# A third matmul and a ScalarE copy in place of VectorE's add, in the first retention of a two-layer language-model tower

## The reference

```python
h = 0                                   # (128 sequences, 128 tokens, 128)
for k in range(3):                      # taps -1, 0, +1
    src = t + k - 1                     # neighbour's place; zero outside the sequence
    h = h + where(valid(src), conv_w[:, :, k].T[ids[:, src]], 0)
h = h + retention(layernorm(h), Wq, Wk, Wv, ...)   # the phase of this case
h = h + experts(layernorm(h), ...)      # top 2 of 8 experts
h = h + complex_retention(layernorm(h), ...)
h = h + merged_experts(layernorm(h), ...)
```

## Time and profile before

| | |
|---|---|
| median of 3 runs | 2128.21 us (2125.86 to 2129.78) |
| the profiled execution | 2130.03 us, its span 2128.3 us |
| TensorE, matmuls | 1922.6 us busy, 90% |
| VectorE | 1511.5 us, 71% |
| ScalarE | 1330.7 us, 63% |
| GpSimd | 1194.4 us, 56% |
| first retention | from the start to about 690 us |

### The profile page before, as it was taken

One profiled execution on the slowest core, in us unless ns is written; L12 is line 12 of the kernel. 1 busy time (PEld: TensorE's weight loads), 2 busy tenths in 40 slices (PEclk: granted clock), 3 DMA queues, 4 the chain that ended last, 5 costly groups with the idle time before them and its releaser, 6 DMA issues. The chain is left out here.

```text
span 2128.3 us, 59058 instructions
## 1 busy us (share of the span) xinstructions
PE 1922.6 (90%) x19932; PEld 1434.3 (67%) x19932; DVE 1511.5 (71%) x4436; ACT 1330.7 (63%) x2940; POOL 1194.4 (56%) x1544
## 2 busy tenths in 40 slices
PE   5888888888886799999999779999999699999997
PEld 2545544455554577777777657777777599999997
DVE  4978888889886233333333379999998678888877
ACT  3756666666663122222222269999998588899885
POOL 5487887888876677888888711111211033333334
PEclk9999999999996899999999979999999899999999
DMA  3122222122211655555555413111110011111111
GB/s 100 39 63 68 66 65 68 61 68 69 65 50 40 183 163 160 159 160 162 161 163 163 134 65 134 40 39 39 39 39 11 16 36 42 41 41 41 42 41 36
DMA packets 113823, 168.80 MB, mean 79 GB/s; under 512 B 19234, under 2 KB 66747, under 8 KB 113572
## 3 DMA queue, kind: packets, MB, share of 16 engines
q1 hardware_dynamic: 87940, 105.09, 17.6%
q0 software_dynamic: 25760, 62.09, 9.1%
HBM read 121.79 MB, written 45.32 MB: 79 GB/s over the span
## 5 line engine op out<-in xcount | busy, mean ns | idle before, releaser
L1277 ACT ACTIVATE b_hT<-b_hbank,b_w 128x512 f32<-128x512 f32 (+1 forms) x156 | 98.2, 630 | 321.1 <-PE b_hbank L1247 321.1
L1221 POOL DMA_INDIRECT done<-b_y,b_row x270 | 263.5, 976 | 48.8 <-issue 45.0
L353 POOL DMA_INDIRECT sent<-a_xn_mid,a_pos_cur x256 | 258.8, 1011 | 47.1 <-issue 43.6
L1303 DVE TENSOR_SCALAR b_hT<-b_hbank,b_w 128x512 f32<-128x512 f32 (+1 forms) x156 | 105.7, 678 | 223.5 <-PE b_hbank L1247 223.5
L1257 PE MATMUL b_bank<-b_w,b_hT 128*128 128x128 f32 x2160 | 255.9, 277 | 1.0 <-DVE b_hT L1303 1.0
L1257 PEld LDWEIGHTS b_bank<-b_w,b_hT 128*128 128x128 f32 x2160 | 249.1, 193 | 1.2 <-DVE b_hT L1303 1.2
L1247 PE MATMUL b_hbank<-b_xT,b_w 128*128 128x512 f32 (+1 forms) x624 | 246.5, 538 | 0.8 <-ACT b_xT L1284 0.8
L1495 POOL TENSOR_TENSOR c_k_early<-c_xn,const_k_decay 64x512 f32<-64x512 f32 x32 | 40.7, 1272 | 332.1 <-ACT c_xn L1703 332.1
L361 POOL TENSOR_TENSOR tv<-tv 128x64 f32<-128x64 f32 x368 | 136.0, 370 | 67.3 <-DVE a_pos_cur L903 56.3
L1247 PEld LDWEIGHTS b_hbank<-b_xT,b_w 128*128 128x128 f32 x624 | 113.5, 192 | 86.9 <-issue 82.5
L1220 POOL TENSOR_TENSOR b_spacer<-b_fill 128x192 f32<-128x192 f32 x266 | 137.8, 518 | 53.1 <-DVE b_y L1311 42.5
(11 more groups left out here) (249 smaller groups left out, 4487.7 us busy)
## 6 DMA issues: line engine op xcount, KB each, us to landing
b_w<-pack_dram SPq DMA_DIRECT2D x78, 258.0 KB
b_w<-pack_dram SPq DMA_DIRECT2D x78, 256.0 KB, 3.1
c_rows<-done SPq DMA_DIRECT2D x32, 512.0 KB, 3.8
b_x<-sent SPq DMA_DIRECT2D x57, 260.0 KB, 2.7
d_b_all<-b_rows SPq DMA_DIRECT2D x32, 256.0 KB, 3.5
out_dram<-h_all SPq DMA_DIRECT2D x32, 256.0 KB, 2.3
b_b<-pack_dram SPq DMA_DIRECT2D x78, 64.5 KB
tv<-tv_dram SPq DMA_DIRECT2D x1, 4736.0 KB, 16.4
```

What stands on the lines that cost most here:

```text
L353: pool.indirect_dma_start(out=sent_d, out_offset=bass.IndirectOffsetOnAxis(ap=pos_cur[:, g.par, b, k:k + 1], axis=0), in_=xn_mid[:, g.par, ...
L1221: pool.indirect_dma_start(out=done_d, out_offset=bass.IndirectOffsetOnAxis(ap=row[:, s.k, j:j + 1], axis=0), in_=y[:, s.par, j, :], in_off ...
```

## The change

The token's own part is added by a third matmul with the identity matrix, in the same PSUM accumulation, and the sum is only copied to `h_all`. The copy is ScalarE's, in the second place of its step; VectorE's `h_sum` is gone. `h_ready` is now raised by the copy. `normalise` takes the four sequences in reverse order. The gather is untouched: it stays three groups ahead.

```diff
@@ tok (TensorE)
                 nc.tensor.matmul(work[0][:], shift_dn, rows[:, g.par, :, 0:D], start=True, stop=False)
-                nc.tensor.matmul(work[0][:], shift_up, rows[:, g.par, :, 2 * D:3 * D],
+                nc.tensor.matmul(work[0][:], shift_up, rows[:, g.par, :, 2 * D:3 * D], start=False, stop=False)
+                nc.tensor.matmul(work[0][:], ident, rows[:, g.par, :, D:2 * D],
                                  start=False, stop=True).then_inc(tok_made, 1)
@@ ScalarE
+            def h_copy(g):
+                act.wait_ge(tok_made, g.n + 1)
+                nc.scalar.activation(h_all[:, bass.ds(g.n * GB, GB), :], work[0][:].rearrange("p (b d) -> p b d", b=GB),
+                                     ACT.Copy).then_inc(h_ready, 1)
+
@@ normalise
-                for b in range(GB):
+                for b in reversed(range(GB)):
@@ step (ScalarE)
                 if g := s.at(0):
                     k_square(g)
+                if g := s.at(2):
+                    h_copy(g)
                 if g := s.at(0):
                     k_std(g)
@@ VectorE
-            def h_sum(g):
-                dve.wait_ge(tok_made, g.n + 1)
-                v.tensor_tensor(h_all[:, of_group(g), :], work[0][:].rearrange("p (b d) -> p b d", b=GB),
-                                rows[:, g.par, :, D:2 * D], ALU.add).then_inc(h_ready, 1)
-
@@ step (VectorE)
-                if g := s.at(2):
-                    h_sum(g)
```

## The result

| | before | after |
|---|---|---|
| median, same chip | 2127.03 us (2124.74 to 2129.78) | 2149.67 us (2146.85 to 2151.30) |
| the profiled execution, its span | 2130.03, 2128.3 | 2151.07, 2149.4 |
| TensorE, matmuls | 1922.6 busy | 1955.0 busy |
| VectorE | 1511.5 | 1493.2 |
| ScalarE | 1330.7 | 1351.5 |

The changed kernel is slower: ratio 1.0109, 95% interval 1.0093 to 1.0125, 22.6 us by the medians and 21.1 by the spans. In the spans the added time lies here: the first waiting `tok` starts at 113.56 instead of 107.53 (+6.0); the 25 steps from it take 516.7 us instead of 501.9 (+14.8); what follows differs by 0.3 at most.

What follows compares the result with a forecast made beforehand. The prediction took the first retention's loop to be bound by a two-step chain from `tok` through `place_tokens` and the gathers. Start 6.7, loop 5.0 and end 0.9 make 12.6: 2142.6 profiled, 2141 as a median, range 2133 to 2152.

Steps and rivals of the forecast that it cites:

- the forecast's own mechanism: First retention's loop: the third matmul lengthens the gathers' two-step chain by 0.93 a pair; 2137 to 2146, chance 0.46.
- the rival of the clock: Loop: 1.2 GHz stretches behind `tok` stay as frequent or grow; 2147 with six low pairs, 2157 with all; chance 0.24.
- The start, +6.7: Steps before the first bound gather: added matmul and `h_copy`'s table load cost 6.7 us, 3.0 in the first step.
- The third matmul's 0.93 on c: Loop: c, from `tok`'s start (T) to `place_tokens`, grows by 0.93; `q_proj` at T+2.7 to 2.8, `qa` at T+3.8.
- `h_sum`'s removal gains nothing: VectorE's step in the loop: the 0.69 us add sat in a wait for TensorE; gain on the path: nothing.
- `h_copy` is hidden: ScalarE, between `k_square` and `k_std`: the 0.6 us copy ends before `qa` starts, or still ahead of the gate.
- The loop, +5.0: 25 steps: 506.9 instead of 501.9, two pairs of steps at 41.85 and 10.5 at 40.3; waits shrink by about 0.2.
- Low stretches behind `tok` in two pairs: Loop: only the first two gather waits, over 3 us, bring 1.2 GHz behind `tok`; those pairs take 41.85.
- GpSimd gave nothing back: Rival, GpSimd's queue: q, from `place_tokens` to the last gather's end, falls by up to 0.9; 2134, chance 0.14.
- the matmul was not free: Rival, loop: the added matmul costs nothing as gathers are late anyway; only the first step's 3 us remain; 2131, chance 0.09.
- VectorE was not the bound: Rival, loop: VectorE's own work is the bound, `h_sum`'s removal saves 0.60 a step; 2116 or 2124, chance 0.07.
- The end, +0.9: Behind the loop: the last group's `tok` lengthens one more c, from `tok` to `place_tokens`, by 0.9 us.

Runs made afterwards that it cites:

- copy_first: The changed kernel with `h_copy` ahead of `k_square` in ScalarE's step; 2148.35 us on the first chip, ratio 1.0104 to the kernel before.
- no_own_tap: The changed kernel without its third matmul, so the token's own part is left out of the sum; 2196.04 us on the second chip, ratio 1.0062 to before.
- ahead4_more: The kernel before with its gathers issued four groups ahead instead of three; 2112.84 us on the first chip, ratio 0.9941.
- late_filler: The kernel before with a useless 128x512 matmul late in the step, behind `place_tokens`; 2145.25 us on the first chip, ratio 1.0096.
- before_again: The kernel before, unchanged, run on the second chip; 2186.57 us, ratio 0.9994.
- after_again: The changed kernel, unchanged, run on the second chip; 2210.74 us, ratio 1.0107 to the kernel before.

## Why the prediction was right, and where it was not

The sign and the range held (2141, 2133 to 2152; measured 2149.67). That the range held is in part luck: the time lies outside the 2137 to 2146 that I gave the forecast's own mechanism, and inside the range only because that made room for the rival of the clock. The added time was 22.6 us where the forecast had 12.6 by its sum, and nearly all of the difference is one term: by the spans the start has 0.7 less than forecast, the loop 9.8 more and the end about 0.6 less.

- **The start, +6.7: measured +6.0.** Its parts were less right than their sum. The first step was to cost 3.0 and cost 1.2 (11.84 to 24.65, against 11.49 to 23.13). The third matmul took 1.47 rather than 1.84, and the load for the copy is paid for by another: the square root's own load, on the path before, now runs at 18.88 while VectorE makes the statistics from 18.99, and the root waits 0.15 instead of the whole load. I counted the new load and not what became of the old one. The next two steps cost 2.9 (forecast 2.6), the three after them 1.6 (forecast 1.1), and 0.35 lay ahead of the first `tok`. The Trainium skill (ScalarE: Activation LUTs, what ACT_TABLE_LOAD costs) would add a drain to each load; the copy starts 0.02 behind its load and the root 0.15, so no run here shows it.
- **The third matmul's 0.93 on c, `qa` at T+3.8, `q_proj` at T+2.7: right.** c is 17.91 at the full clock, `q_proj` stands at T+2.68 (198.08), `qa` at T+3.87 in the step from 217.37. The pair is 40.23 (forecast 40.3).
- **`h_sum`'s removal gains nothing: right.** VectorE's `qa` waits 3.10 us for TensorE in that step, and in each of the 25 (51.0 us in all), so a VectorE that is done earlier only waits longer there. Its work fell by 12 us in the loop (436 to 425).
- **`h_copy` is hidden: right in the loop on the chip of the forecast** (none of the engines waits for it there, and copy_first moves it without effect). In the start VectorE's statistics wait for it (18.99, above). On the second chip no_own_tap costs 11 us, of which the copy may be a part.
- **The loop, +5.0: measured +14.8. This is the step that failed.** The forecast said that the work between two `tok`s grows by 0.93 and 0.2 and that "the wait shrinks by about 0.2", so that every pair stays the chain's pair. I never priced TensorE's own step without the wait. ahead4_more gives it as 19.33 before, and the changed loop as about 20.3, no shorter than the 20.15 of half a pair, and uneven. So only 5 of the 25 steps end in a wait for a gather, where 12 did before. late_filler shows it from the other side: a matmul that no gather waits for, which by the forecast's chain costs nothing, makes the loop 8.0 longer. That is half of the 14.8; how the rest divides is open.
- **Low stretches behind `tok` in two pairs: wrong in place, and wrong in what they go by.** The two waits that stayed long, 3.12 and 3.33, were to have them and did not; the one that came stands behind a wait of 1.87, at 524.00. So the length of the wait does not decide it, as the forecast took it to do on both sides of 1.82. Fifteen more came late in the step, where the kernel before has six that the forecast did not count. The rival "the clock stays low as often as now, or more often" (2147) came nearest in time, by another mechanism than it described: the late stretches do not lengthen c (17.8 to 18.2 in their steps, 19.8 in the one that also has one behind `tok`), they lengthen TensorE's own step. Of the other rivals none is seen: GpSimd gave nothing back (q is 20.15 in the turn shown, between the 19.91 and 20.35 of before), the matmul was not free, and VectorE was not the bound.
- **The end, +0.9: measured 0.3 at most** for all that follows, within what single executions differ.

What stays open: what makes the clock fall late in one step and not in the next, how the 14.8 divide between the matmul as work and as a link of the chain, and why the changed kernel without its matmul still costs 11 us on the second chip. The order in which `normalise` takes its blocks was not tried by itself.

The one version that beats both kernels is the kernel before with its gathers four groups ahead: 2112.84 us, ratio 0.9941 on the first chip, 0.9968 on the second.

## What to carry to other kernels

Where a loop is bound by a chain with a wait in it, price the busy engine's own step as well: take its step without the wait, at the clock that it then gets, and compare it with the chain. Here the wait of 1.9 us in every second step looked like slack for two matmuls, and the true distance was 0.75 us a step, less than one. And when an edit adds a table load, look at what happens to the next load: the two can trade places on the path.

## What was not expected of the hardware

- The granted clock of TensorE fell in the same part of the step again and again without a wait for a DMA there, in 6 of 25 steps before and in 15 after. It stayed at 1.00 behind a DMA wait of 3.33 us in one kernel and fell behind one of 1.89 in the other. The mean clock of the loop went from 0.96 to 0.93 with one more matmul and to 0.98 with two.
- The second chip is 58 to 60 us slower with the same kernel, and its loop differs in kind. The window of before_again's loop and a piece of its timeline:

```profile
107.00:657.00 550.00, 456.15 (x3783) 271.29 (x3771) 438.30 (x1453) 332.44 (x754) 420.81 (x629) 0.89 0.20 60
...
375.27 1.06 PE L527 MATMUL a_bank<-a_gate_w,a_xT_mid 128*128 128x8 f32 x8
376.19 1.11 PE L424 MATMUL a_bank<-a_xT,a_wqs 128*128 128x512 f32 x2
378.92 0.19 DVE L854 TENSOR_TENSOR a_lg<-a_bank,a_gate_c 128x32 f32<-128x32 f32 x1 [3.04 <-remote]
379.26 0.93 PE L449 MATMUL a_bank<-a_wkkv,a_xT 128*128 128x384 f32 x2 [1.96 <-DVE a_lg L854]
```

`gate_sum` starts 2.6 us after the gate's last matmul (375.27+1.06 = 376.33), where on the first chip it starts at once (0.77 of idle in all), and TensorE stands still behind it. In before_again it starts 1.8 to 4.2 us late in 22 of the 25 steps and 0.8 in the others, in after_again 1.6 to 4.6 in all 25; on the first chip it never starts more than 0.13 late, in either kernel. Nothing in the trace says what is waited for. That the ratio is the same on both chips, 1.0109 and 1.0107, is therefore no proof that the causes are.
